# Retention and routed transformer on eight cores: PSUM bank rotation, the place of a count, three output tiles begun early, a last tile in two parts

## The reference

```python
xn = layernorm(x)                                     # x: 4 x 2048 x 2048, float32
q, k, v = split(xn @ w_qkv); q, k = xpos(q), xpos(k)  # 16 heads of 128
y = (q @ k.T * 128**-0.5 * decay_mask) @ v            # retention, no softmax
s = (silu(xn @ w_g) * groupnorm(y)) @ w_proj
d = argmax(xn @ w_router.T)                           # 3 paths, for each token
out0 = xn + simple_bias
out1 = xn + xn @ w_down.T @ w_up.T
h  = xn + softmax_attention(layernorm(xn)) @ wo.T     # causal, 16 heads
out2 = h + gelu(layernorm(h) @ w_ff1.T) @ w_ff2.T     # 2048 -> 8192 -> 2048
g = silu(where(d == 0, out0, where(d == 1, out1, out2)))
out = x + s * g
```

## Time and profile before

| | |
|---|---|
| three runs, median (lowest, highest) | 2000.48 us (1982.11, 2228.18) |
| the profiled execution, its own time | 1997.9 us |
| its span, slowest core (6) | 1996.0 us |
| spans of the even cores 0, 2, 4, 6 | 1989.9, 1991.2, 1985.3, 1996.0 us |
| spans of the odd cores 1, 3, 5, 7 | 1964.5, 1971.1, 1953.3, 1955.0 us |
| TensorE busy on core 6 | 1760.5 us (88%) |
| VectorE, ScalarE, GpSimd busy | 898.6 (45%), 690.7 (35%), 183.8 us (9%) |

### The profile page before, as it was taken

How to read it: one execution, slowest core, us unless ns; L and a number is a source line. 1 busy time by engine, 2 the same in 40 slices (tenths; PEclk the granted TensorE clock), 3 DMA queues, 4 the chain that set the end, 5 groups by cost and what they waited for, 6 DMA issues and landing times.

```text
span 1996.0 us, 27121 instructions; the slowest of 8 cores (1953.3 to 1996.0 us)
## 1 busy us (share of the span) xinstructions
PE 1760.5 (88%) x9150; PEld 888.1 (44%) x9274; DVE 898.6 (45%) x1600; ACT 690.7 (35%) x1104; POOL 183.8 (9%) x315
## 2 busy tenths in 40 slices
PE   4977797788978899989999999979978799999996
PEld 2544343444444445544454444434434344445553
DVE  4557776655265534434032777867882400000000
ACT  2323422444244524556252444434541411110000
POOL 0000000000000000001000000000111111112211
PEclk9988998989999999999999999989988999999998
DMA  8598763566555515227364698777859399999992
GB/s 220 153 184 153 172 147 98 124 92 129 164 120 110 118 43 111 59 47 175 81 159 73 147 179 178 137 146 140 175 114 151 59 169 169 168 170 170 168 155 31
DMA packets 128362, 267.34 MB, mean 134 GB/s; under 512 B 16018, under 2 KB 58258, under 8 KB 126930
## 3 DMA queue, kind: packets, MB, share of 16 engines
q0 software_dynamic: 43728, 151.67, 46.1%
q1 hardware_dynamic: 83186, 113.76, 21.4%
q10 hardware_dynamic: 1296, 0.01, 0.0%
HBM read 371.87 MB, written 37.17 MB: 205 GB/s over the span
## 4 chain that ended last, share of the span: by engine, by line
PE 64%; DVE 11%; DMA 10%; issue 7%; ACT 7%; SPq 1%; DVEq 0%; POOL 0%; ACTq 0%; POOLq 0%
PE pM L264 10%; PE pB L264 10%; PE S L264 9%; PE pA L264 9%; PE pB L1809 4%; PE pA L1809 3%; PE pM L1809 3%; ACT L249 2%; DMA a_yx<-xp 2%; PE pA L1251 2%; PE pM L1251 2%; PE pB L1251 2%; DMA a_tab<-tab 2%; DMA a_hk<-xk_sp 2%; DVE S L249 1%
## 5 line engine op out<-in xcount | busy, mean ns | idle before, releaser
L264 PE MATMUL S<-a_xn,a_wr 128*128 128x512 bf16 (+1 forms) x1273 | 261.4, 362 | 7.8 <-DVE a_sc L249 7.2
L264 PEld LDWEIGHTS S<-a_xn,a_wr 128*128 128x128 bf16 x1280 | 130.0, 103 | 121.6 <-issue 30.4
L249 ACT ACT_TABLE_LOAD x66 | 84.7, 1283 | 96.8 <-PE S L264 39.0
L249 ACT ACTIVATE a_er<-S 128x928 bf16<-128x928 f32 x80 | 75.5, 944 | 121.2 <-DVE S L249 120.6
L249 DVE TENSOR_TENSOR S<-S,a_cb 128x928 f32<-128x928 f32 x80 | 89.8, 1127 | 52.8 <-PE S L1477 52.7
L219 POOL DMA_DIRECT2D a_wb<-f x128 | 69.2, 560 | 350.2 <-PE pM L264 50.8
L264 PE MATMUL pB<-a_vw,a_xn 128*128 128x512 bf16 x406 | 92.8, 379 | 1.7 <-DVE a_acc L249 1.2
L264 PE MATMUL pM<-a_xn,a_wr 128*128 128x512 bf16 (+1 forms) x429 | 90.7, 369 | 2.0 <-DVE a_sc L249 1.8
L1796 DVE MEMSET a_fg<- 128x48 bf16 x2 | 0.2, 98 | 188.7 <-PE pA L264 188.7
L249 DVE SCALAR_TENSOR_TENSOR a_rj<-a_rx,mv,a_wrh 128x1024 bf16<-128x1024 f32 x60 | 76.8, 1281 | 15.2 <-DMA a_wrh<-wr 9.0
L264 PE MATMUL pA<-a_vw,a_xn 128*128 128x512 bf16 x298 | 70.3, 389 | 8.3 <-DMA a_vw<-rv 7.9
(11 more groups left out here) (362 smaller groups left out, 3110.5 us busy)
## 6 DMA issues: line engine op xcount, KB each, us to landing
a_wb<-f POOLq DMA_DIRECT2D x128, 512.0 KB, 22.7
a_tab<-tab SPq DMA_DIRECT2D x96, 256.0 KB, 5.3
a_rx<-xp SPq DMA_DIRECT2D x20, 512.0 KB, 6.1
a_yx<-xp SPq DMA_DIRECT2D x40, 256.0 KB, 6.5
out_tok<-a_yx SPq DMA_DIRECT2D x40, 256.0 KB, 5.4
a_vw<-rv POOLq DMA_DIRECT2D x16, 512.0 KB, 10.4
a_wr<-rq POOLq DMA_DIRECT2D x16, 512.0 KB, 6.0
a_wr<-rk POOLq DMA_DIRECT2D x16, 512.0 KB, 7.3
```

What stands on the lines that cost most here:

```text
L249: return self.done(e, f(*args, **kw))
L264: inst = self.nc.tensor.matmul(self.pb[k][:, 0:w], lhs(ct), rhs(ct), start=(ct == 0), stop=(ct == CT - 1))
```

## The change

It makes six edits.

1. `pairs_to_banks` puts Y into the rotation, which then has eight banks. `ret_av` takes a bank for each chunk at its first A, holds it, and gives it back behind the last A.
2. `route` stores `count` in `self.count_slots`, and `ret_vburst` puts it into `pend` behind the three `ret_lr` groups; `h_buffers` waits for `t_msk` instead of `t_pos`.
3. The piece of `vw` is loaded behind main 3 of a head, not ahead of main 0.
4. `ffn_step(15)` begins three output tiles, at p = kp-3, kp-2 and kp-1; `wo` adds X and Z to the rotation (its denominator takes X), and emits a tile's sums between its own start and its finish.
5. `ff2` emits the `finish` of the tile before behind 16 matmuls of the group.
6. The last ff tile is done in two parts by slots, 256 and 208 on an even core, 128 and 160 on an odd one. Each has its own 64 matmuls, addition, silu, transposes, product and stores.

```diff
     def pairs_to_banks(self):
...
-        self.rot += ["C", "D", "X", "Z"]
+        self.rot += ["Y", "C", "D", "X", "Z"]
...
         for u in range(g.on):
-            self.hk_load(u, self.t_pos, *self.t_xk.values())
+            self.hk_load(u, self.t_msk, *self.t_xk.values())
...
-        Y = self.pb["Y"]
         self.wait("pe", t, self.t_v[j], self.t_v[j + 1])
         if skip == 0:
-            self.wait("pe", self.free["Y"], self.t_st)
+            self.avk = self.bank()
+            self.held.add(self.avk)
+        Y = self.pb[self.avk]
+        if skip == 0:
+            self.wait("pe", self.free[self.avk], self.t_st)
...
-            self.free["Y"] = self.t_y[h, c]
+            self.free[self.avk] = self.t_y[h, c]
+            self.held.remove(self.avk)
...
-        if h < 12:
-
-            self.vw_load("rv", h // 4 + 1, self.vw_last, [h % 4])
...
             self.gap(main)
+            if h < 12 and a == 3:
+
+                self.vw_load("rv", h // 4 + 1, self.vw_last, [h % 4])
...
             for c in range(len(self.g.qc)):
                 self.gap(lambda: self.ret_lr(c))
+            self.pend.append(self.count_slots)
             self.h_buffers()
...
-        self.pend.append(count)
+        self.count_slots = count
...
-                if h == 15 and p in (kp - 3, kp - 1):
-                    self.wo_start((p - kp + 3) // 2)
+                if h == 15 and p >= kp - 3:
+                    self.wo_start(p - kp + 3)
...
         self.flush()
+        self.free["X"] = self.free["Z"] = self.Sfree[1]
+        self.rot = ["X", "Z"] + self.rot
         self.ffn_den(15)
-        self.wo_finish(0)
-        self.wo_finish(1)
-        for c2 in range(2, 16):
-            def tile():
-                self.wo_start(c2)
-                self.wo_finish(c2)
-            self.gap(tile)
+        for c2 in range(3):
+            self.wo_finish(c2)
+        for c2 in range(3, 16):
+            self.wo_start(c2)
+            self.flush()
+            self.wo_finish(c2)
...
-        self.wait("pe", *[self.free[k] for k in "ABMY"], *self.Sfree)
+        self.wait("pe", *[self.free[k] for k in "ABMYXZ"], self.Sfree[0])
+        self.rot = [k for k in self.rot if k in "ABM"]
...
-        for c2 in range(16):
-            q, a = c2 // 4, c2 % 2
+        half = nst // 2
+        parts = [(c2, 0, nst) for c2 in range(15)] + [(15, 0, half), (15, half, nst)]
+        for n, (c2, s0, s1) in enumerate(parts):
+            q, a = c2 // 4, n % 2
+            lo, hi = s0 * P, min(sl, s1 * P)
...
+                if ft == 15:
+                    self.flush()
...
-            self.flush()
...
-                for st in range(nst):
+                for st in range(s0, s1):
```

More of the change, by code:

```diff
@@ L1808, in ff2 @@
                 self.wait("pe", self.t_hg[ft])
-                ins = nc.tensor.matmul(self.pb[b][:, 0:sl],
-                                       w[:, (ft % 16) * P:(ft % 16 + 1) * P], self.hg[ft][:, :],
+                ins = nc.tensor.matmul(self.pb[b][:, 0:hi - lo],
+                                       w[:, (ft % 16) * P:(ft % 16 + 1) * P],
+                                       self.hg[ft][:, lo:hi],
                                        start=(ft == 0), stop=(ft == FT - 1))
@@ L1813, in ff2, with finish @@
                     tg = self.done("pe", ins)
-                    self.big.release(key, tg)
-            t = self.op("dve", "tt", z[a][:, :], self.pb[b][:, 0:sl], self.x2[:, c2, :], op=ALU.add,
-                        toks=(tg, z_used[a]))
+                    if s1 == nst:
+                        self.big.release(key, tg)
+                if ft == 15:
+                    self.flush()
+            t = self.op("dve", "tt", z[a][:, lo:hi], self.pb[b][:, 0:hi - lo],
+                        self.x2[:, c2, lo:hi], op=ALU.add, toks=(tg, z_used[a]))
             self.free[b] = t
-            z_used[a] = t_g = self.op("act", "act", g2[a][:, 0:sl], z[a][:, :], AF.Silu,
+            z_used[a] = t_g = self.op("act", "act", g2[a][:, lo:hi], z[a][:, lo:hi], AF.Silu,
                                       toks=(t, g_used[a], t_fill[a]))
-            self.flush()
-            def finish(c2=c2, q=q, a=a, t_g=t_g):
+            def finish(c2=c2, q=q, a=a, s0=s0, s1=s1, t_g=t_g):
                 out = self.S[a].ap().rearrange("p a n -> p (a n)").bitcast(BF16)[:, 0:wide]
                 self.wait("pe", t_g, self.Sfree[a])
-                for st in range(nst):
+                for st in range(s0, s1):
                     ins = nc.tensor.transpose(out[:, st * P:(st + 1) * P],
@@ L1829, in finish @@
                 cols = slice((c2 % 4) * P, (c2 % 4 + 1) * P)
[L1830 to L1833, removed]
+                t = self.op("dve", "tt", y[q % 2][:, s0:s1, cols],
+                            out.rearrange("p (a n) -> p a n", a=nst)[:, s0:s1, :],
+                            self.sg[:, s0:s1, c2 * P:(c2 + 1) * P], op=ALU.mult,
+                            toks=(tp, *self.t_sg, *((y_used[q % 2] or ()) if s0 == 0 else ())))
                 self.Sfree[a] = t
                 if c2 % 4 == 3:
-                    y_used[q % 2] = []
-                    for st in range(nst):
+                    if s0 == 0:
+                        y_used[q % 2] = []
+                    for st in range(s0, s1):
                         n = min(P, sl - st * P)
```

## The result

The kernel after takes 1970.12 us (median of 19 runs, from 1958.45 to 2209.76), the kernel before beside it 1992.78 us (19 runs). The ratio is 0.990, 95% interval 0.988 to 0.993: 19 us, within the 2% that count as no change. The forecast was 1973 us and "within 2%", with 27 us for the sum. So the sum was too large by two fifths (26.8 for 19), and the forecast time fits as well as it does by luck: the profiled execution of before, 1997.9 us, from which the sum was taken, was a long one, 9 us above the mean. (In some executions one die or both run longer at a lower granted clock; ratios and means leave these out, medians do not.)

A forecast was written before the change was run, and what follows sets the result against it. Even core 6 was taken to set the time, with TensorE's idle time mostly short retention waits. Terms -5, -11, -4, -2.4 and -4.4 sum to -26.8 us on 1997.9, giving 1971; forecast 1973 us, range 1957 to 1995.

The forecast's parts named there:

- A(2) ... gets the very bank that A(1) has just given back: Retention, heads 1 to 3 and 12 to 14: A(2) still waits for the same copy; head 12's 2.17 us stay.
- the -5 of the sum: Retention: the forecast total for putting bank Y into the rotation, -5 us.
- U ... moves ahead of a wait ... half a microsecond in each of eight heads: Retention, gaps 1 to 3: with the longer list U no longer waits for VectorE; -4 us, between 0 and -10.
- the waits for Y really go: Rival, retention: the 38.4 us of waits vanish on even cores, odd cores then set the time at 1968 us; 6%.
- they gain only what comes before it; their 1971.1 would be about 1966: Odd cores: from 930 us on they wait for the ff weight stream, so their floor is about 1966 us.
- The count: Router, before head 4: moving the count's matmuls removes TensorE's idle time and low clock there; -11 us, between -8 and -12.
- The wait goes, with nothing left over: Count's ten sums: 9.2 us of matmuls placed before them cover the 8.69 us that TensorE idles.
- The vw pieces: Heads 1 to 11, later vw loads: head 2 -3, head 3 +3, waits for small loads -4; sum -4 us.
- The rival from the Trainium skill's rule of arbitration: vw loads: DMA engines alternate between queues, so the move is worth nothing where queues are full anyway; 1977 us, 18%.
- The last head: Last head and wo: three tiles begun before the denominator stall, X and Z added to the rotation; -2.4 us, between +1 and -5.
- The tail: End of ff: earlier finish and last tile in two parts, with two stores left at the end; -4.4 us, -1 to -6.
- a store's landing takes the tail's gain: End of the kernel: named sign of a wrong forecast, the landing of a store using up the -4.4 us.

The follow-up runs named there:

- b_back: The kernel after, but a bank that AV gives back goes to the end of the rotation; ratio 0.980 to the kernel before, even cores -45.1 us.
- u_rot: The kernel after with the rotation change undone (bank Y for all AV); ratio 0.992 to the kernel before, even cores -17.0 us.
- r_after: The kernel after, unchanged, timed again; ratio 0.992 to the kernel before, even cores -21.9 us, odd -9.5.
- p_count: The kernel before with only the count's matmuls put behind the other lr groups and `t_msk` for `t_pos`; ratio 0.999, even cores -4.1 us.
- p_rot: The kernel before with only Y put into the rotation and AV taking its bank from it; ratio 1.003, even cores +7.2 us, odd -24.1.
- p_rotvw: The kernel before with Y in the rotation and the vw pieces loaded later; ratio 1.001, even cores -0.7 us, odd -13.9.

## Why the prediction was right, and where not

**The rotation.** The step "A(2) ... gets the very bank that A(1) has just given back" is shown twice: by the 1.95 us that stay and by b_back, where two added lines take them away. The 4.9 us of edit 1 within the whole change are the -5 of the sum, but that is in part luck. Head 15 gives 2.3 of them, for -2. The main term, "U ... moves ahead of a wait ... half a microsecond in each of eight heads", -4, is not found: U's wait for `a_sc` does go, and in heads 5 to 11 waits for `a_sc` fall from 15.3 us a core in u_rot to 12.7 in r_after, yet these heads get no shorter (338.5 and 341.5 us). Where the other 2.6 us come from is open. The step was read from S(1) and U alone; the same shift of the list by one gave Q2 a bank of the h products. Edit 1 alone cost the even cores 7 us. I had looked for a loss only in a group that waits for a just released bank; here it was a bank released by an operation that waits for a transfer.

**The rival "the waits for Y really go"** was priced at 1968 us: 33 us more on the even cores, with the odd cores as floor. In b_back, in which they do go, the even cores gain 23 us on the kernel after, and the time is 1940 us. The floor failed in "they gain only what comes before it; their 1971.1 would be about 1966". The odd cores gained 24 us from edit 1 alone, in the retention and just behind it, and the longest one in the profile after has 1952.2 us.

**The count.** -11 was forecast: 8 us at head 4 in p_count (11 with edit 3 in both kernels, 97.0 and 86.0 us), 4 kept at the end, 2.23 us of wait left in the kernel after. "The wait goes, with nothing left over" holds for the sums on 15 of the 36 even cores profiled with edit 2; on the others 0.2 to 3.3 us are left, in kernels with and without edit 3, since the cover of 9.2 us was set against the 8.69 us of one core, and core 2 had 9.9. What failed is that a gain at head 4 counts in full: of the 8 us the even cores kept 4.

**The vw pieces.** -4 forecast, -2.8 measured, head 2 and head 3 with the signs named (-5 and +3 for -3 and +3). The rival from the Trainium skill's rule of arbitration ("DMA: Bandwidth & Descriptors", section "Queues, rings and completion order") gave 0 for it; 2.8 us with an error of 1.3 leans to the forecast and does not firmly exclude it. Where edit 1 stands, the same move is worth 8 us (p_rot to p_rotvw, error 2), so that it is worth nothing is excluded there.

**The last head.** -2.4 forecast, 95.4 to 92.8 us measured. Not seen: the first to the last gelu of ff is another 1.7 us shorter (179.0 to 177.3), in the kernels with this edit. Its cause is open.

**The tail.** -4.4 forecast, 0 measured. "The last at 1984.89; now two are issued under the second part" is right, -3.4 us at the issue. The term that failed is what lies behind the issue, left out of the sum as if it stayed at 11.1 us; it is 14.3. The prediction named this as a sign of being wrong, "a store's landing takes the tail's gain", and so it is. The lower bound, "-1 (the accumulating stores collide)", was the nearer value.

**The sum.** With the terms measured (edit 1 -5, edits 2 and 3 -8.5, last head -2.6 and -1.7, tail -0.4) it would have been -18. These are means of the even cores, so the measure to hold them against is the -21.9 of r_after; the 4 us between are the ones left unexplained above. The forecast sum of -26.8 is 5 us beyond that measure and 8 beyond the time of the slowest core.

## What to carry to other kernels

A list of buffers that rotate by order of calls does not by itself keep a buffer that is held for long from coming to the front as it is released. Count the calls between release and next use; where they make a full round, append on release. That this helps is shown for this kernel alone. The Trainium skill, "Perfetto Trace Analysis", section "Matmuls", says to rotate independent groups through the PSUM banks so that their evacuations overlap the next group; edit 1 does that and alone cost 0.3%; in the kernel after, the other order of release took another 1.2% off (ratio 0.980 for 0.992).

For each user that a longer list shifts, ask who empties the bank it now gets, and what that engine itself waits for. And where cores run the same code on other sizes, read the wait before the moved instruction on each kind: the split tile was neutral on one and cost 9 us on the other.

## What was not expected of the hardware

An accumulating store that GpSimd issues among loads of weights lands up to 91 us after its issue on the odd cores and up to 29 us on the even ones, about as late as the loads around it, and after 4 to 5 us on the odd cores once the loads are done. The last store of the even cores lands after 7.1 to 8.3 us in all eight profiles with the split tile and after 4.5 to 6.7 us in the six without; on the odd cores there is no such difference (3.7 to 5.4 us). The cause is open. Behind the last landing the program needs 5.7 to 7.2 us more to its end on the even cores and 2.8 to 3.0 us on the odd ones.
